# Reordering the opening of a gated attention kernel: K(2) ahead of score(1), a copy given to VectorE, and loads and stores moved between the queues

## The chip, the cores and the metric

The kernel runs on one core of one Trainium2 chip. The metric is the time of one execution on the device in microseconds (us), the median over several executions; lower is better. Engine names in the profile: PE is TensorE, with PEld for its weight loads, DVE is VectorE, ACT is ScalarE, POOL is GpSimd, SP is the engine that here only issues DMAs.

## The reference, cut to what matters

`x` and `ctx` are 4 x 512 rows of 512 numbers, float32. Attention here runs over the 16 heads of one and the same token, not over tokens: for every token a 16 x 16 score matrix is formed.

```python
def attn(q, k, v):                       # 16 heads of 32
    Q = (q @ Wq.T + bq).reshape(bs, sl, 16, 32)
    K = (k @ Wk.T + bk).reshape(bs, sl, 16, 32)
    V = (v @ Wv.T + bv).reshape(bs, sl, 16, 32)
    weight = softmax(einsum('bshd,bsgd->bshg', Q, K), axis=-1)
    return einsum('bshg,bsgd->bshd', weight, V).reshape(bs, sl, 512) @ Wo.T + bo

x = x + tanh(g_xattn[0]) * attn(layernorm(x), ctx, ctx)
w = weight * scale_weight[:, None]
x = x + tanh(g_ffn[0]) * (layernorm(x) @ w.T + bias)
```

## The kernel before, in words

**Tiling.** The 2048 rows are cut into eight chunks of 256 tokens, c = 0 to 7, each of two tiles of 128. Every layer product (K, Q, V, O for the output projection, F for the last layer) keeps float32 precision by splitting both factors into a high and a low part in fp32r: `hi` is the rounded value, `lo` the difference. ScalarE makes the high parts (`high`, L718), VectorE or GpSimd the low ones (`low`, L911). A product is high x high, then the two mixed terms, 12 matmuls per output block. K and Q come out transposed (`cols_layer`, L510: two blocks of two groups, 48 matmuls of 256 columns), V, O and F as rows (`rows_layer`, L499: two tiles of 12 matmuls of 512 columns). All of them share the two PSUM banks `acc[0]` and `acc[1]`: a layer may start on a bank only when the layer before has been read out of it (`bank_free`, L480).

**Per chunk.** K and Q are written to DRAM scratch and read back in another layout (`save_k`, `load_k`, `save_q`, `load_q`, L324 to L352), K is laid out once more by ScalarE (`lay_keys`, L781), V goes through DRAM too (`save_v`, `load_v`, L368 to L384). `score(c)` (L606) is 128 small matmuls and needs the loaded Q and the laid K. VectorE then turns the scores and does the softmax (`scores_turn`, `softmax_a`, `softmax_b`), with the exponential on ScalarE, and `spread_first` (L1034 on) spreads the weights over a block diagonal; GpSimd or ScalarE does the rest of the spread. `attend(c)` (L624) is 128 small matmuls on it. Their result is copied out of PSUM in 16 copies of 32 x 256, 8 for each tile (`attn_copy`, L787, ScalarE; for the last chunk VectorE helps in `attn_some`, L1059), split into high and low (`attn_high`, `attn_low`), and used by O. `o_residual` (L1079) adds the residual and frees the bank; it waits for the output bias that GpSimd adds to the residual rows (`res_bias`, L1250). The layer norms are `norm_stats` and `norm_apply` on VectorE with a small power on GpSimd (`root`, L1239); `turn_x1` and `turn_x2` transpose their results on TensorE.

**Order.** Each engine has its own instruction stream, and the order in it is written out by hand: a prologue, then `tensor_step(i)`, `scalar_step(i)`, `vector_step(i)` and `pool_step(i)` for i = 0 to 8, steps 2 to 5 in a loop. An engine works strictly in its order; a wait holds up all that is behind it. The engines meet at semaphores only. The parts that matter here:

- TensorE (L652 to L703): 12 warming matmuls, K(0), V(0) with the transposes of x(0) between its tiles, Q(0), half of K(1), the transposes of x(1), the rest of K(1), half of Q(1). Step 0: score(0), the rest of Q(1), V(1), attend(0), transposes of x(2). Step 1: score(1), K(2), O(0), Q(2), attend(1), transposes of x2(0), V(2), F(0). O(0) puts its result into the banks that K(2) has left, Q(2) takes the banks that O(0) has left, F(0) those that V(2) has left.
- ScalarE (L821 to L904): in step 0 exp(0), half of Q(1)'s bias, the issue of Q(1)'s store (L872), the spread, ctx(2)'s high part, lay_keys(1), tanh, x(2)'s high part, copies of attention(0)'s first tile and its high part, half of K(2)'s bias; in step 1 the copies of the second tile come first.
- VectorE, `second_step` (L1116 on): scores and first half of softmax(1), low part of attention(0)'s tile 0, the two bias rows multiplied by tanh, second half of the softmax, x(2)'s low part, attention(0)'s tile 1, the spread, o_residual(0) and the second layer norm, the scaling of the F weights, norm of x(3), `x1_apply(3)` (L945), the low parts of F's weights and of x2(0), then `v_bias(2)` (L990), which frees the bank for F(0).
- GpSimd (`pool_step`): in step 0 the root for x(2) and `res_bias(0)`, which waits for both scaled bias rows; in step 1 `spread_last(1)`, two roots, one more root, `x2_bias(0)`, which waits for both low parts of x2(0), `res_bias(1)`, ctx(3)'s low part.
- SP (L400 to L437): all loads and stores, in one queue in written order.

## Time and profile before

| | |
|---|---|
| median of 3 runs | 281.3 us |
| lowest and highest | 280.01 and 281.74 us |
| the profiled execution's own time | 281.8 us |
| its span in the trace | 280.1 us |
| TensorE matmul busy | 267.5 us, 96% of the span |
| VectorE, ScalarE, GpSimd busy | 198.8, 144.5 and 88.4 us |
| DMA | 53.83 MB, mean 192 GB/s |

The profiled execution lies 0.5 us above the median, and 1.7 us of its time lie outside the span. Times in rows are from the span's start. A row of a timeline gives the start, the time from first start to last end, the engine, the line, the instruction, what it writes and reads, how often, and in brackets how long the engine had been idle before and what ended that.

### The profile page before, as it was taken

To read this page: it belongs to the slowest core of one execution; us is meant where nothing else is said; L and a number is where in the kernel's file an instruction comes from. 1 tells how busy PE (TensorE), PEld (TensorE's weight loads), DVE (VectorE), ACT (ScalarE), POOL (GpSimd) and SP (SyncE) were. 2 spreads that over 40 slices of the span, in tenths; PEclk is the share of its full clock that TensorE was granted. 3 is DMA by queue.
4 is the path that set the end of the run, shared out by engine and by line. 5 is a ranking of instruction groups with operands and counts; after the bars stand their busy time and mean duration, and the time that the engine had idled before them with its cause. 6 is when DMAs were issued, how large, how long until landed. Compare 5 with 4: busy or idle time off the path is not lost.

```text
span 280.1 us, 8653 instructions
## 1 busy us (share of the span) xinstructions
PE 267.5 (96%) x3516; PEld 235.9 (84%) x3516; DVE 198.8 (71%) x331; ACT 144.5 (52%) x276; POOL 88.4 (32%) x80
## 2 busy tenths in 40 slices
PE   7899998498999999999999999999999999999995
PEld 7789997397978898888988899889988998887775
DVE  2775569189885987569774987579773855598884
ACT  4755543853686236643387225933289432954700
POOL 4104000032157116422183024612183031802722
PEclk9999999899999999999999999999999999999999
DMA  6997769991887764894488853986478729263203
GB/s 204 351 382 226 208 247 249 258 232 56 274 248 237 147 225 150 235 220 139 160 232 247 191 195 130 240 225 156 181 201 246 158 77 231 74 128 72 104 37 112
DMA packets 71912, 53.83 MB, mean 192 GB/s; under 512 B 36688, under 2 KB 59984, under 8 KB 71888
## 3 DMA queue, kind: packets, MB, share of 16 engines
q1 hardware_dynamic: 71744, 52.97, 65.6%
q10 hardware_dynamic: 144, 0.52, 0.5%
q8 instruction: 17, 0.28, 0.4%
q14 instruction: 7, 0.06, 0.1%
HBM read 34.08 MB, written 19.40 MB: 191 GB/s over the span
## 4 chain that ended last, share of the span: by engine, by line
PE 69%; DMA 10%; SPq 7%; ACT 7%; DVE 3%; issue 3%; DVEq 0%; ACTq 0%
PE acc L496 55%; PE score_ps L496 4%; PE score_ps L616 3%; DMA raw_spare<-wq_t 3%; ACT late L796 3%; PE attn_ps L638 3%; PE turn_ps L530 2%; DMA v_scratch<-v_or_norm 2%; SPq L350 2%; DMA k_rows<-k_scratch 2%; DMA q_pad<-q_scratch 2%; SPq L398 1%; SPq L335 1%; DVE turned L1002 1%; DMA q_scratch<-q_t 1%
## 5 line engine op out<-in xcount | busy, mean ns | idle before, releaser
L796 ACT ACTIVATE late<-attn_ps 32x256 f32<-32x256 f32 x124 | 46.6, 376 | 6.1 <-PE attn_ps L638 3.2
L496 PE MATMUL acc<-ctx_parts,wk_parts 128*128 128x256 f32 x384 | 48.7, 285 | 0.3 <-DVE late L1079 0.2
L496 PEld LDWEIGHTS acc<-ctx_parts,wk_parts 128*128 128x128 f32 x384 | 47.1, 191 | 1.7 <-issue 0.8
L1242 POOL TENSOR_TENSOR rstd<-var_eps,minus_half 128x1 f32<-128x1 f32 (+1 forms) x24 | 17.5, 728 | 95.3 <-DVE var_eps L937 95.3
L496 PE MATMUL acc<-wv_parts,ctx_parts 128*128 128x512 f32 x192 | 46.0, 394 | 0.8 <-ACT wv_parts L720 0.8
L496 PEld LDWEIGHTS acc<-wv_parts,ctx_parts 128*128 128x128 f32 x192 | 35.4, 188 | 8.1 <-issue 1.0
L496 PE MATMUL acc<-xa_parts,wq_parts 128*128 128x256 f32 x336 | 41.1, 281 | 0.1
L496 PE MATMUL acc<-wo_parts,xa_parts 128*128 128x512 f32 x168 | 40.4, 395 | 0.6 <-ACT xa_parts L720 0.6
L496 PEld LDWEIGHTS acc<-xa_parts,wq_parts 128*128 128x128 f32 x336 | 40.2, 188 | 0.7 <-DVE xa_parts L913 0.5
L496 PEld LDWEIGHTS acc<-wo_parts,xa_parts 128*128 128x128 f32 x168 | 31.0, 188 | 7.9 <-ACT xa_parts L720 1.0
L496 PE MATMUL acc<-wf_parts,x_parts 128*128 128x512 f32 (+1 forms) x132 | 29.7, 380 | 0.1
L770 ACT ACTIVATE q_t<-acc,bq_col 128x256 f32<-128x256 f32 x32 | 13.4, 470 | 29.6 <-PE acc L496 29.5
L496 PEld LDWEIGHTS acc<-wf_parts,x_parts 128*128 128x128 f32 x132 | 24.0, 188 | 5.2 <-issue 0.5
L1253 POOL TENSOR_TENSOR x_res<-x_res,bo_row 128x512 f32<-128x512 f32 x16 | 22.0, 1397 | 17.0 <-DVE bf_row L1123 16.8
L1266 POOL TENSOR_TENSOR spread<-probs_t,same_token 128x768 f32<-128x768 f32 x6 | 10.1, 1685 | 49.2 <-DVE probs_t L1032 49.2
L770 ACT ACTIVATE k_t<-acc,bk_col 128x256 f32<-128x256 f32 x32 | 13.3, 471 | 21.5 <-PE acc L496 21.3
L784 ACT ACTIVATE k_keys<-k_rows 128x1024 f32<-128x1024 f32 x8 | 16.5, 2062 | 12.8 <-DMA k_rows<-k_scratch 12.8
L1071 DVE SCALAR_TENSOR_TENSOR late<-acc,tanh_g,late 128x512 f32<-128x512 f32 (+1 forms) x11 | 8.0, 726 | 18.3 <-PE acc L496 18.3
L1247 POOL TENSOR_TENSOR ctx_parts<-ctx_raw,ctx_parts 128x1024 fp32r<-128x1024 f32 x6 | 14.5, 2425 | 19.0 <-ACT ctx_parts L720 19.0
L1259 POOL TENSOR_TENSOR late<-late,bf_row 128x512 f32<-128x512 f32 x14 | 19.1, 1380 | 4.5 <-DVE x_parts L913 3.5
L1002 DVE STREAM_TRANSPOSE turned<-score_ps 128x512 f32<-128x512 f32 x16 | 10.5, 694 | 11.9 <-PE score_ps L616 11.6
L751 ACT ACTIVATE probs<-probs 128x512 f32<-128x512 f32 x8 | 5.1, 632 | 23.8 <-DVE probs L1017 23.8
(89 smaller groups left out, 377.7 us busy)
## 6 DMA issues: line engine op xcount, KB each, us to landing
ctx_raw<-ctx_t SPq DMA_DIRECT2D x8, 512.0 KB, 4.7
x_norm<-x SPq DMA_DIRECT2D x8, 512.0 KB, 5.2
k_scratch<-k_t SPq DMA_DIRECT2D x8, 512.0 KB, 3.7
k_rows<-k_scratch SPq DMA_DIRECT2D x32, 128.0 KB, 3.4
q_pad<-q_scratch SPq DMA_DIRECT2D x32, 128.0 KB, 3.2
v_scratch<-v_or_norm SPq DMA_DIRECT2D x32, 128.0 KB, 2.2
v_keys<-v_scratch SPq DMA_DIRECT2D x16, 256.0 KB, 4.3
x_res<-x SPq DMA_DIRECT2D x8, 512.0 KB, 3.8
```

What stands on the lines that cost most here:

```text
L496: last = pe.matmul(dst, left(a, k), right(b, k), start=(n == 0), stop=(n == len(terms) - 1))
L616: last = pe.matmul(score_ps[r][HD * pair:HD * (pair + 1), ROWS * o:ROWS * (o + 1)], k_keys[half, n:n + 2].rearrange("p s g -> p (s g)"), q ...
L638: last = pe.matmul(attn_ps[HD * t:HD * (t + 1), BANK * r + ROWS * eight:BANK * r + ROWS * (eight + 1)], v_keys[half, EIGHTS * t + eight, : ...
L770: nc.scalar.activation(dst[:, :, m, :], acc[m // 2][:, TOK * (m % 2):TOK * (m % 2 + 1)].rearrange("p (t n) -> p t n", t=GROUPS), ACT.Ident ...
L784: nc.scalar.activation(k_keys[:].rearrange("p n (m q) -> p n m q", q=QH), k_rows[:].rearrange("p q m n -> p n m q"), ACT.Identity).then_in ...
L796: nc.scalar.activation(attn_rows(t, q), attn_block(t, q), ACT.Identity).then_inc(a_out, 1)
L1002: nc.vector.transpose(by_half[:, b].rearrange("p e (s x) -> p e s x", s=2), score_ps[b][:].rearrange("p (e x s) -> p e s x", x=HT, s=2)).t ...
L1242: nc.gpsimd.tensor_tensor(rstd[which][:, t], var_eps[which][:, t], minus_half[:, t], ALU.pow).then_inc(n_rstd[which], count)
L1247: nc.gpsimd.tensor_tensor(ctx_parts[:, LO], ctx_raw[:], ctx_parts[:, HI].bitcast(F32), ALU.subtract).then_inc(ctx_lo, 1)
L1253: nc.gpsimd.tensor_tensor(x_res[:, t, :], x_res[:, t, :], bo_row[:], ALU.add).then_inc(res_biased, 1)
L1259: nc.gpsimd.tensor_tensor(x2_of(c)[:, t, :], x2_of(c)[:, t, :], bf_row[:], ALU.add).then_inc(x2_biased, 1)
L1266: nc.gpsimd.tensor_tensor(spread[:, first:].rearrange("p o h t -> p (o h) t"), probs_t[:, first:].rearrange("p o h -> p (o h)").unsqueeze( ...
```

## The change

It has six parts.

1. TensorE: K(2) runs ahead of score(1), behind the transposes of x(2), where it was behind score(1).
2. Attention(0)'s second tile is copied out of PSUM by VectorE (8 copies), in VectorE's step 0. ScalarE copies the first tile as before, and then lays K(1), takes x(2)'s high part, K(2)'s bias and the second tile's high part, all in step 0.
3. Start: x(0) is loaded behind the two halves of wv. VectorE takes x(0)'s statistics behind the low parts of wv. The transposes of x(0) stand 4 matmuls inside V(0)'s second tile. Q(0) waits for x(0)'s high part at its start, and for the low part at the first term with it.
4. ScalarE issues V(0)'s four stores and, later, its two loads; SP issues Q(1)'s store, which was ScalarE's. On SP K(1)'s store and loads stand before ctx(2)'s load.
5. The two bias rows are loaded behind Q(1)'s loads, and VectorE multiplies them with tanh behind softmax(1), directly ahead of the spread.
6. F(0): the low part of its weights is waited for inside the first tile; on VectorE the low parts of x2(0)'s tiles stand around that of the second half of F's weights, and `x1_apply(3)` stands behind all of them, ahead of `v_bias(2)`.

```diff
@@ groups_of
+            if first(c):
+                owner = "act" if tile == 0 else "dve"
+                return range(tile * each, (tile + 1) * each) if engine == owner else ()
@@ SP
-            load_x(0)
             for j in range(2):
                 load_w(WV, j)
+            load_x(0)
...
             save_k(0)
             load_x(1)
-            for row, dram in ((bo_row, bo), (bf_row, bf)):
-                sp.dma_start(row[:], dram.partition_broadcast(P)).then_inc(consts_in, DMA)
             load_k(0)
             save_q(0)
             sp.wait_ge(zeroed, 1)
             load_q(0)
+            save_k(1)
             load_x(2)
+            load_k(1)
             load_ctx(2)
-            save_v(0)
-            save_k(1)
-            load_v(0)
-            load_k(1)
+            save_q(1)
             load_q(1)
+            for row, dram in ((bo_row, bo), (bf_row, bf)):
+                sp.dma_start(row[:], dram.partition_broadcast(P)).then_inc(consts_in, DMA)
             load_res(0)
@@ TensorE
-                    if t_done and t == 1:
-                        t_done()
...
+                def within(t):
+                    if t_done and t == 1:
+                        t_done()
+                rows_layer(ctx_parts, "wv", v_mm, high_ready, within,
...
-                    pe.wait_ge(x1_lo, TILES * (c + 1))
+                    pe.wait_ge(x1_hi if first(c) else x1_lo, TILES * (c + 1))
...
+                    if first(c) and t == 0:
+                        pe.wait_ge(w_hi, pieces_to(WF, 1))
...
+                if first(i - 1):
+                    k_layer(2, "v", 1)
                 score(i)
...
                 elif first(i - 1):
-                    k_layer(2, "v", 1)
@@ ScalarE
             for j in range(3):
                 w_high(WK, j)
+            w_high(WV, 0)
             act.wait_ge(biases_in, 2 * DMA)
             k_bias(0, (0,))
-            w_high(WV, 0)
...
             ctx_high(1)
+            act.wait_ge(v_out, TILES)
+            for half in range(2):
+                for r in range(2):
+                    part = 2 * half + r
+                    act.dma_start(v_halves(0)[r].rearrange("(t h n) d -> h n t d", t=TILES, h=2)[half],
+                                  v_rows[HD * part:HD * (part + 1)]).then_inc(v_saved, DMA)
             q_bias(0, (0,))
...
             q_bias(1, (0,))
+            act.wait_ge(v_saved, V_SAVED)
+            for r in range(2):
+                act.dma_start(v_keys[ROWS * r:ROWS * (r + 1)], v_halves(0)[r].rearrange(
+                    "(o e) (g d) -> (e g) o d", e=ROW_TOK, d=HD)).then_inc(v_in, DMA)
...
                     q_bias(1, (1,))
-                    act.wait_ge(q_out, KC * 2)
-                    act.wait_ge(q_moved, DMA * GROUPS)
-                    act.dma_start(q_scratch[:], q_t[:].rearrange("p t m n -> p (t m n)")).then_inc(q_saved, DMA)
                     spread_some(i)
                     ctx_high(2)
-                    lay_keys(1)
                     act.wait_ge(gates_in, 2 * DMA)
                     nc.scalar.activation(tanh_g[:], gates[:], ACT.Tanh).then_inc(gates_done, 1)
-                    x1_high(2)
                     attn_copy(0, 0)
                     attn_high(0, 0)
-                    k_bias(2, (0,))
+                    lay_keys(1)
+                    x1_high(2)
+                    k_bias(2)
+                    attn_high(0, 1)
                     return
-                if first(i - 1):
-                    attn_copy(0, 1)
-                    attn_high(0, 1)
-                    k_bias(2, (1,))
@@ VectorE
                 v_bias(1, 0)
+                ctx_low(2)
                 v_bias(1, 1)
-                ctx_low(2)
+                attn_some(0, 1)
+                attn_low(0, 0)

             def second_step():
                 scores_turn(1)
                 softmax_a(1)
-                attn_low(0, 0)
+                attn_low(0, 1)
+                turned_lo(xa_parts, x1_hi, x1_lo, 2)
+                softmax_b(1)
                 dve.wait_ge(consts_in, 2 * DMA)
                 dve.wait_ge(gates_done, 1)
                 for row, n in ((bo_row, 0), (bf_row, 1)):
                     nc.vector.tensor_scalar(row[:], row[:], tanh_g[:, n:n + 1], None, ALU.mult).then_inc(rows_scaled, 1)
-                softmax_b(1)
-                turned_lo(xa_parts, x1_hi, x1_lo, 2)
-                attn_low(0, 1)
                 spread_first(1)
...
                 w_low(WF, 0)
+                turned_lo(x2_parts, x2_hi, x2_lo, 0, (0,))
+                w_low(WF, 1)
+                turned_lo(x2_parts, x2_hi, x2_lo, 0, (1,))
                 x1_apply(3)
-                w_low(WF, 1)
-                turned_lo(x2_parts, x2_hi, x2_lo, 0)
                 v_bias(2, 0)
```

The counts of ScalarE's and VectorE's copies that later waits compare with are shifted to match.

## Rows read from the trace of the kernel before

**Rows 1.** Timeline of TensorE: start us, us, instruction, count

```profile
13.71 2.97 PE L496 MATMUL acc<-wv_parts,ctx_parts 128*128 128x512 f32 x12 [0.80 <-ACT wv_parts L720]
...
20.36 5.90 PE L496 MATMUL acc<-xa_parts,wq_parts 128*128 128x256 f32 x48
...
46.74 1.50 PE L638 MATMUL attn_ps<-spread,v_keys 64*32 64x64 f32 x128 [0.92 <-DMA v_keys<-v_scratch]
...
53.42 1.95 PE L616 MATMUL score_ps<-q_pad,k_keys 64*32 64x64 f32 x128 [4.16 <-DMA q_pad<-q_scratch]
55.30 6.71 PE L496 MATMUL acc<-ctx_parts,wk_parts 128*128 128x256 f32 x48
...
68.38 5.80 PE L496 MATMUL acc<-xa_parts,wq_parts 128*128 128x256 f32 x48
...
76.40 5.74 PE L496 MATMUL acc<-wv_parts,ctx_parts 128*128 128x512 f32 x24
82.23 5.71 PE L496 MATMUL acc<-wf_parts,x_parts 128*128 128x512 f32 x24
87.87 1.59 PE L616 MATMUL score_ps<-q_pad,k_keys 64*32 64x64 f32 x128
```

**Rows 2.** Windows: stretch, length, busy us by engine, PE clock, DMA share, GB/s

```profile
49.30:53.40 4.10, 0.00 (x0) 0.01 (x1) 0.16 (x1) 3.75 (x7) 0.00 (x0) 1.00 1.06 284
...
55.40:57.00 1.60, 1.60 (x8) 1.60 (x9) 1.57 (x3) 0.87 (x2) 0.00 (x0) 0.50 0.93 261
```

**Rows 3.** DMA issues of the first 95 us: count, KB, median us to landing

```profile
x_norm<-x SPq DMA_DIRECT2D x5, 512.0 KB, 5.6
```

**Rows 4.** Timeline of GpSimd, four stretches

```profile
12.71 1.54 POOL L1242 TENSOR_TENSOR rstd<-var_eps,minus_half 128x2 f32<-128x2 f32 x1 [8.66 <-DVE var_eps L937]
...
26.28 0.70 POOL L1242 TENSOR_TENSOR rstd<-var_eps,minus_half 128x2 f32<-128x2 f32 x1 [2.35 <-DVE var_eps L937]
...
59.63 2.53 POOL L1253 TENSOR_TENSOR x_res<-x_res,bo_row 128x512 f32<-128x512 f32 x2 [16.82 <-DVE bf_row L1123]
...
81.56 3.06 POOL L1259 TENSOR_TENSOR late<-late,bf_row 128x512 f32<-128x512 f32 x2 [3.45 <-DVE x_parts L913]
...
108.68 2.72 POOL L1259 TENSOR_TENSOR late<-late,bf_row 128x512 f32<-128x512 f32 x2
```

**Rows 5.** Timeline of VectorE, four stretches

```profile
12.47 2.35 DVE L913 TENSOR_TENSOR wv_parts<-late,wv_parts 128x1024 fp32r<-128x1024 f32 x2
...
44.46 1.76 DVE L1041 TENSOR_TENSOR spread<-probs_t,same_token 128x1536 f32<-128x1536 f32 x1
...
55.39 1.31 DVE L1002 STREAM_TRANSPOSE turned<-score_ps 128x512 f32<-128x512 f32 x2 [5.93 <-PE score_ps L616]
...
65.48 1.48 DVE L1049 TENSOR_TENSOR spread<-probs_t,same_token 128x1280 f32<-128x1280 f32 x1
66.88 0.74 DVE L1079 SCALAR_TENSOR_TENSOR late<-acc,tanh_g,x_res 128x512 f32<-128x512 f32 x1
...
78.15 1.00 DVE L950 TENSOR_SCALAR raw_spare<-x_norm,moments,rstd 128x512 f32<-128x512 f32 x2 [0.59 <-POOL rstd L1242]
...
80.20 1.28 DVE L913 TENSOR_TENSOR x_parts<-turn_ps,x_parts 128x512 fp32r<-128x512 f32 x2
81.40 1.46 DVE L996 TENSOR_TENSOR v_or_norm<-acc,bv_row 128x512 f32<-128x512 f32 x2
...
108.75 2.93 DVE L950 TENSOR_SCALAR raw_spare<-x_norm,moments,rstd 128x512 f32<-128x512 f32 x2 [0.88 <-POOL rstd L1242]
```

**Rows 6.** Timeline of ScalarE

```profile
49.60 1.93 ACT L784 ACTIVATE k_keys<-k_rows 128x1024 f32<-128x1024 f32 x1 [2.62 <-DMA k_rows<-k_scratch]
...
76.08 3.14 ACT L796 ACTIVATE late<-attn_ps 32x256 f32<-32x256 f32 x8
79.25 1.09 ACT L720 ACTIVATE x_parts<-turn_ps 128x512 fp32r<-128x512 f32 x2
```

**Rows 7.** Operations on attn_ps: count, ns minimum, median, maximum, first and last start

```profile
L1065 DVE COPY late<-attn_ps x4: 419/421/423, 259.6 to 261.0; 32x256 f32<-32x256 f32 x4
```

27 lines of the change are left out of this document (16 added, 11 removed).

## The prediction

> **What bounds the kernel now.** I began with the table of busy shares (TensorE 96% of the span) and the waits of TensorE. Its largest is that of score(1) on Q's loads. The timeline of TensorE places it: attend(0) starts at 46.74 after 0.92 idle, score(1) at 53.42 after 4.16, and at the start V(0) had waited 0.80 [rows 1]. From F(0) at 82.23 on, TensorE works almost without a gap to the end, so what counts is one number: when F(0) starts. The windows show a second price of the long wait: the clock reads 1.00 while TensorE idles and 0.50 (1.2 GHz) after it resumes [rows 2]. Score(1) took 1.95 instead of 1.59, K(2) 6.71 instead of the 5.80 of Q(2), of the same shape [rows 1]: 0.36 + 0.91 = 1.3 us.
>
> Then the engines that feed it. The landing of x is 5.6 us [rows 3]. GpSimd and VectorE read differently together than apart: the root at 12.71 took 1.54 us beside VectorE's low parts (from 12.47), the one at 26.28 only 0.70; and `x1_apply` took 1.00 us at 78.15 with GpSimd idle, 2.93 at 108.75 beside the 2.72 of `x2_bias` from 108.68 [rows 4, 5]. One of the two stands still behind the other. Last, ScalarE (lay_keys 1.93, 8 copies 3.14 [rows 6]) and a copy on VectorE (0.42 [rows 7]).
>
> **Start (parts 3, 4).** x(0), issued behind wv, gives wv the queue: half a megabyte less ahead of it. I take V(0)'s 0.80 wait as gone, V(0) at 12.95. VectorE takes x(0)'s statistics only behind the low parts of wv, about 14.0 instead of 10.6. Statistics 2.0 (10.6 to the root at 12.71), root 0.70 (VectorE is idle now [rows 4]), first apply 0.55 with latencies: about 17.5. TensorE has done tile 0 and four matmuls at 16.7 (12 matmuls are 2.8 us [rows 1]), so it waits 0.8 there. Q(0) starts at 20.3 against 20.36 [rows 1]. The sum of the start is 0; ends: -0.7 if x lands early and nothing waits, +0.9 if the root takes 1.54 again.
>
> ScalarE's six DMA issues lie where it waited before (V(0)'s store, from 22.8, up to the bias of Q(0), the loads behind Q(1)'s first half). I take nothing, bounds 0 and +0.5, from a store's issue of 0.4 us four times against about 1 us of free time. V(0)'s loads leave at about 37 and, with the 5.6 of x for a landing [rows 3], are there at 43. Then attend(0) waits for the spread alone, 44.46 + 1.76 = 46.22 [rows 5]: it starts at 46.27, gain 0.47. Bounds 0 and 0.92 [rows 1].
>
> **K(2) ahead of score(1) (parts 1, 2).** From Q(2)'s start to V(2)'s are 8.02, of which Q is 5.73 and attend with its transposes 2.29 [rows 1]; so K(2) can start at 46.27 + 2.29 = 48.56. It needs ctx(2)'s high part, which ScalarE makes when V(1) has ended (46.74 - 0.92 = 45.8), about 1.1 long like the 1.09 of as many elements [rows 6]: 47.1 with latencies. VectorE's low part follows (1.2, half of 2.35 [rows 5]), now ahead of V(1)'s second bias: 48.9, used at 49.0. K(2) runs at full clock, 5.7: 54.25. Score(1) needs lay_keys(1): copies from 47.8 (attend(0)'s end), 3.14, high part 0.6, lay_keys 1.93 [rows 6] = 53.5, covered by 0.7. VectorE's eight copies at 0.445 from start to start are 3.6 [rows 7], 49.5 to 53.1, in a hole of 5.93 us [rows 5]: free. Score(1) takes 1.5: it ends at 55.8 instead of 55.4.
>
> So the 4.16 wait, 1.3 of clock and 0.47 are removed and K(2)'s 5.7 us are done earlier. But Q(2) needs the bank that `o_residual(0)` frees, and that hangs on the softmax of score(1). Before, K(2) and O(0) covered it; now O(0) alone. O(0) ends at 61.4. VectorE, from score(1)'s end: transposes, peak, subtraction 2.7; low parts 1.8; second softmax half 2.5; both bias rows 0.8: 7.8 in all, each link with its start-to-start time of the same timeline, so the spread starts at 63.6. Before, from the transposes at 55.39 to the spread at 65.48 were 10.1 [rows 5]; 1.2 less of waiting for exp and about 1 of waiting behind GpSimd make up the difference.
>
> **The bias rows (part 5).** GpSimd may add the bias to the residual only when both rows are scaled. Before, that was at 59.6, 7 us ahead of use [rows 4, 5]. Now it comes at the moment at which the spread starts on VectorE. If GpSimd stands still behind the spread (1.48 [rows 5]), as the root did behind the low part at 12.5, then half of 2.53 = 1.27 [rows 4] follows: `o_residual(0)` starts at 63.6 + 1.48 + 1.27 + 0.1 = 66.4, else at 65.0. With its 0.74 Q(2) starts at 67.2, against 68.38 before: 1.2 earlier is all that is left. TensorE has then been idle for 5.8 us. The only long idle time in the trace dropped the clock, so I add a slow stretch again: 1.6 (bounds 0.9, what K(2) lost alone, and 1.8, half of the 3.6 us from 53.42 [rows 1] to 57.0, up to where the window shows 0.50 [rows 2]). Q(2) ends at 74.5, against 74.11: +0.4.
>
> At 12.71 VectorE had started first and GpSimd was the one held: 12.47 + 1.18 + 0.6 = 14.25, just the end of its 1.54. The Trainium skill ("SBUF — State Buffer", section "Who interferes with whom") says the same for two kinds of VectorE instructions, those with two SBUF inputs and the fast single-input modes, and that the second to start blocks fully. By that rule the sum is the one here, and 1.3 lower at Q(2) without it.
>
> **F(0) (part 6).** Before, the eight copies of attention(1)'s first tile started 1.97 behind Q(2)'s end (76.08 [rows 6] less 68.38 + 5.73). Now: 74.5 + 1.8 = 76.3, the ends of q_bias and of F's second high part, no idle time between. Copies 3.14, first half of 1.09 [rows 6] with latency 0.6: x2(0)'s first high part at 80.0. Before, VectorE used this time for `x1_apply(3)` (78.15) and F's second low part, and v_bias(2) came right behind x2(0)'s low parts, at 81.40 [rows 5]. Now VectorE idles from about 77 to 80 and then has in front of v_bias(2): 0.6 + 1.15 + 0.65 = 82.4, and `x1_apply(3)`. The second low part of x2(0) is also what releases GpSimd's `x2_bias` (81.56, right behind 80.20 + 1.28 [rows 4, 5]). So `x1_apply(3)` and `x2_bias(0)` start together: 1.0 alone, 2.93 at worst [rows 5]; one of the two tiles held is 2.1 (1.0 and one `x2_bias` tile of 1.36, less some 0.3 that VectorE's own first tile covers), which I take. v_bias(2) 0.7: F(0) starts at 82.4 + 2.1 + 0.7 = 85.2. The ends are 84.1 and 86.1. V(2) has ended at 82.5; a wait of 2.7 stands ahead of F(0), where 0.09 was. Waits of 0.9 kept the clock and 4.16 lost it, so here it may fall too: 0 to +1.2, taken as 0.
>
> **Sum.** F(0) starts at 85.2 against 82.23: +3.0. Nothing behind it gets shorter; x(3) goes to DRAM 2 to 3 us later, with slack of about as much until VectorE turns it, taken as 0. The profiled execution would become 281.8 + 3.0 = 284.8; it lies 0.5 above the median, so 284.3 as a median of runs, 1.1% slower. About 1% is what a measurement of this kernel can tell from no change.
>
> **Rivals.**
> A. No collision: GpSimd does not hold the residual up, `x1_apply(3)` takes 1.0, the clock falls little. Q(2) then starts at 65.9 and ends at 71.7 to 73.3, the copies at 74.4 to 75, high part at 78.2 to 78.7, F(0) at 82.2 to 82.7. 0 to +0.5: 281.3 to 281.8, no change. For it: at both places the two start within some 0.1 to 0.2 us of each other (GpSimd at 81.56, where the VectorE rows end at 81.48), so a little decides. Against it: in the rows GpSimd and VectorE lengthen each other every time they meet.
> B. The saving stays: what is removed (4.16 + 1.3 + 0.47 = 5.9) is not given back, or half of it, 278 to 275.4. It decides if `o_residual(0)` is ready within 6 us of score(1)'s end; for it speaks that 11.5 us of the old order (55.39 to 66.88 [rows 5]) held work that has moved away. Against it: what is left there is a chain of 9 us on one engine.
> C. ctx(2) or K(1) comes late. ctx(2)'s load is now behind K(1)'s loads, about 39.5, where it was at 32. Landing of the same size is 5.6 [rows 3], 45.1, against a need at 46. Beyond 46.6 it moves score(1) nearly one for one, and all behind it. At 2 us late: 286.
>
> **How the numbers follow.** Forecast 0.55, A 0.22, B 0.10, C 0.13. The forecast's own spread is F(0) from 84.1 to 86.1 and 0.5 for score(1), 282.8 to 286.0; 0.36 of its 0.55 lies above 284.1, the 1% line. Slower by over 1%: 0.36 + 0.11 of C = 0.47. Faster: B, 0.10. Within: 0.43. The range 280.6 to 286.4 leaves out B and the far end of C and of the slow clock, 0.2 in all.
>
> **What would show it.** Right: no wait ahead of score(1) and K(2) ahead of it; a wait of 5 to 6 us of TensorE ahead of Q(2), released by VectorE's L1079, and the clock at 0.50 after it; `res_bias(0)` longer than 2.53; `x1_apply(3)` at 1.5 to 2.9 and a wait of 2 to 3 us ahead of F(0). Wrong: Q(2) before 66, or F(0) before 83.5. The start is judged by Q(0) at 20.3, C by ScalarE's high part of ctx(2) later than 46.6.

## The result, and the profile after

| | before | changed |
|---|---|---|
| median, first comparison | 280.83 us (280.01 to 281.74, 4 executions) | 289.35 us (287.01 to 291.13, 4 executions) |
| ratio, 95% interval | | 1.0281 [1.0233, 1.0329] |
| the profiled execution, its span, mean clock | 281.8, 280.1 us | 287.01, 285.3 us, 0.988 |

The changed kernel is 2.8% slower, where 1.1% had been predicted: the sign is right, and the time lies 3 us above the range. The same kernel was measured twice more, beside the experiments: 285.63 us, 1.0167 [1.0120, 1.0214], and 285.95 us, 1.0176 [1.0115, 1.0236]. So a loss of some 1.7% came back each time, inside the predicted range, and about 1% was there in the first comparison alone. A ratio leaves out every execution more than 1.5% above the fastest of its kernel, so below it can differ from the quotient of two medians.

The mean granted clock of the single executions explains a part of this. The kernel before ran 279.1 to 279.9 us at a mean clock of 1.00 and, but for two executions of 284.2 and 286.6, 280.8 to 283.2 at 0.988; one more, of 327.2 at 0.754, stands apart. The changed one, in its twelve executions, ran 284.6 to 286.4 at 0.999 and 1.00, 285.0 to 287.0 at 0.988, 288.0 at 0.982, and 287.1, 290.7 and 291.1 at 0.975 and 0.976. So 5 to 7 us are there at the same full clock, and in some executions a clock that fell in more stretches comes on top. The mean clock does not settle a time by itself: at 0.975 and 0.976 the times still lie 4 us apart.

The timeline of TensorE of the changed kernel (columns as in [rows 1]):

```profile
13.50 3.87 PE L502 MATMUL acc<-wv_parts,ctx_parts 128*128 128x512 f32 x16
17.96 1.11 PE L536 MATMUL turn_ps<-ident,x_norm 128*128 128x128 f32 x8 [0.60 <-DVE x_norm L984]
...
20.76 6.07 PE L502 MATMUL acc<-xa_parts,wq_parts 128*128 128x256 f32 x48
...
47.62 1.50 PE L652 MATMUL attn_ps<-spread,v_keys 64*32 64x64 f32 x128 [1.07 <-DMA v_keys<-v_scratch]
...
49.89 5.88 PE L502 MATMUL acc<-ctx_parts,wk_parts 128*128 128x256 f32 x48
55.71 1.59 PE L628 MATMUL score_ps<-q_pad,k_keys 64*32 64x64 f32 x128
57.23 1.67 PE L502 MATMUL acc<-wo_parts,x_parts 128*128 128x512 f32 x6
60.57 4.38 PE L502 MATMUL acc<-wo_parts,x_parts 128*128 128x512 f32 x18 [1.68 <-issue]
68.63 7.45 PE L502 MATMUL acc<-xa_parts,wq_parts 128*128 128x256 f32 x48 [3.68 <-DVE late L1098]
...
86.59 7.08 PE L502 MATMUL acc<-wf_parts,x_parts 128*128 128x512 f32 x24 [2.58 <-issue]
93.60 1.59 PE L628 MATMUL score_ps<-q_pad,k_keys 64*32 64x64 f32 x128
```

Against [rows 1]: attend(0) starts 0.88 later (47.62 for 46.74) and waits 1.07 for `v_keys` where it waited 0.92; K(2) and score(1) run without a wait; the 4.16 us wait of before has become one of 3.68 ahead of Q(2) and one of 2.58 ahead of F(0), with a stop of 1.68 inside O(0) besides. F(0) starts 4.36 later (86.59 for 82.23) and takes 1.37 longer, so score(2) starts 5.73 later. Of that the rest of the kernel gives back half a microsecond: the span is 5.2 longer.

Most of the 0.88 is older than attend(0). VectorE's spread, which attend(0) needs too, starts at 45.15 for 44.46 [rows 5], 0.69 later, and ScalarE's last high part of wk had started 0.78 later, ahead of all that the change moved (first the kernel before, then the changed one):

```profile
8.37 1.06 ACT L720 ACTIVATE wk_parts<-spread 128x1024 fp32r<-128x1024 f32 x1 [0.78 <-DMA spread<-wk_t]
```

```profile
9.15 1.06 ACT L733 ACTIVATE wk_parts<-spread 128x1024 fp32r<-128x1024 f32 x1 [0.75 <-DMA spread<-wk_t]
...
45.15 1.76 DVE L1060 TENSOR_TENSOR spread<-probs_t,same_token 128x1536 f32<-128x1536 f32 x1
```

That part of `wk` starts anywhere from 8.12 to 9.82 in the profiles below, and Q(0) from 20.13 to 21.41; in the second repeat of the changed kernel Q(0) starts at 20.14.

The windows behind the two waits, columns as in [rows 2], show the clock falling both times:

```profile
68.60:70.00 1.40, 1.37 (x8) 1.40 (x9) 1.21 (x4) 0.00 (x0) 1.40 (x2) 0.64 0.22 72
70.00:72.00 2.00, 2.00 (x11) 2.00 (x11) 1.77 (x5) 0.00 (x0) 1.03 (x3) 0.50 0.22 24
...
86.60:88.00 1.40, 1.40 (x3) 1.12 (x4) 1.40 (x2) 1.33 (x4) 1.40 (x2) 0.50 0.82 320
```

0.50 is the 1.2 GHz level. Q(2) took 7.45 us instead of 5.80, F(0) 7.08 instead of 5.71.

GpSimd of the changed kernel, against [rows 4]. The root of x(0) no longer meets VectorE (0.71 for 1.54); `res_bias(0)` now meets the spread (3.66 for 2.53):

```profile
16.62 0.71 POOL L1263 TENSOR_TENSOR rstd<-var_eps,minus_half 128x2 f32<-128x2 f32 x1 [12.56 <-DVE var_eps L956]
...
65.18 3.66 POOL L1274 TENSOR_TENSOR x_res<-x_res,bo_row 128x512 f32<-128x512 f32 x2 [21.68 <-DVE bf_row L1146]
...
84.10 2.92 POOL L1280 TENSOR_TENSOR late<-late,bf_row 128x512 f32<-128x512 f32 x2 [5.12 <-DVE x_parts L932]
```

VectorE of the changed kernel, against [rows 5]. `o_residual(0)` waits 1.23 for GpSimd; `x1_apply(3)` starts 0.16 ahead of GpSimd's `x2_bias(0)` and takes 1.96 instead of 1.00, with `v_bias(2)`, which frees F(0)'s bank, right behind it:

```profile
65.02 1.48 DVE L1068 TENSOR_TENSOR spread<-probs_t,same_token 128x1280 f32<-128x1280 f32 x1
67.73 0.75 DVE L1098 SCALAR_TENSOR_TENSOR late<-acc,tanh_g,x_res 128x512 f32<-128x512 f32 x1 [1.23 <-POOL x_res L1274]
...
81.59 0.69 DVE L932 TENSOR_TENSOR x_parts<-turn_ps,x_parts 128x512 fp32r<-128x512 f32 x1 [3.17 <-ACT x_parts L733]
...
83.94 1.96 DVE L969 TENSOR_SCALAR raw_spare<-x_norm,moments,rstd 128x512 f32<-128x512 f32 x2
85.81 1.27 DVE L1015 TENSOR_TENSOR v_or_norm<-acc,bv_row 128x512 f32<-128x512 f32 x2
```

So the wait ahead of F(0), which the timeline calls "issue", is one for `v_bias(2)`'s first half: F(0) follows 0.78 behind its start.

The DMA queues and issues from 30 to 48 us (queue: packets, MB, share of the 16 engines; then count, KB, median us to landing):

```profile
q1 hardware_dynamic: 2243, 3.14, 59.0%
q10 hardware_dynamic: 4128, 0.52, 20.0%
...
v_keys<-v_scratch ACTq DMA_DIRECT2D x2, 256.0 KB, 8.4
k_rows<-k_scratch SPq DMA_DIRECT2D x4, 128.0 KB, 4.7
ctx_raw<-ctx_t SPq DMA_DIRECT2D x1, 512.0 KB, 8.1
```

Queue q10, ScalarE's, carries V(0)'s half megabyte in 4128 packets, some 127 bytes each, beside q1, SP's. The two loads left at 36.4 and 37.1 and the slower one landed after 10.3 us, at 47.5. Before, SP issued them 4 us later, at 40.4, and they landed after 3.7 and 5.4. They were sent earlier and arrived later.

### The profile page after: what moved, and what is told of

It is laid out like the page before. It is cut to its first block, busy times and chain, and to the rows that moved or that the text cites. A ratio compares the mean times of both kernels' runs of the same rounds, so it can differ in the third digit from the quotient of the medians.

```text
span 285.3 us, 8652 instructions
## 1 busy us (share of the span) xinstructions
PE 269.8 (95%) x3516; PEld 238.1 (83%) x3516; DVE 203.1 (71%) x339; ACT 141.5 (50%) x268; POOL 88.7 (31%) x80
## 4 chain that ended last, share of the span: by engine, by line
PE 77%; DMA 7%; issue 4%; DVE 4%; ACT 3%; SPq 2%; POOL 1%; DVEq 0%; POOLq 0%; ACTq 0%
PE acc L502 62%; PE score_ps L502 4%; PE score_ps L628 4%; PE attn_ps L652 4%; PE turn_ps L536 3%; DMA x_res<-x 3%; DMA late<-wv_t 2%; DMA q_scratch<-q_t 2%; ACT late L809 1%; SPq L342 1%; DVE turned L1021 1%; POOL x_res L1274 1%; ACT k_t L783 1%; SPq L405 1%; DVE peak L1033 1%
## 5 line engine op out<-in xcount | busy, mean ns | idle before, releaser
L502 PE MATMUL acc<-ctx_parts,wk_parts 128*128 128x256 f32 x384 | 47.9, 283 | 0.1
L502 PEld LDWEIGHTS acc<-ctx_parts,wk_parts 128*128 128x128 f32 x384 | 46.6, 189 | 0.9 <-ACT wk_parts L733 0.3
L809 ACT ACTIVATE late<-attn_ps 32x256 f32<-32x256 f32 x116 | 43.6, 376 | 6.5 <-PE attn_ps L652 3.9
L502 PE MATMUL acc<-xa_parts,wq_parts 128*128 128x256 f32 x336 | 42.8, 287 | 3.7 <-DVE late L1098 3.7
L1263 POOL TENSOR_TENSOR rstd<-var_eps,minus_half 128x1 f32<-128x1 f32 (+1 forms) x24 | 16.7, 695 | 95.0 <-DVE var_eps L956 95.0
L502 PEld LDWEIGHTS acc<-xa_parts,wq_parts 128*128 128x128 f32 x336 | 41.8, 195 | 4.4 <-issue 4.1
L502 PE MATMUL acc<-wf_parts,x_parts 128*128 128x512 f32 (+1 forms) x132 | 31.1, 392 | 2.6 <-issue 2.6
L502 PEld LDWEIGHTS acc<-wf_parts,x_parts 128*128 128x128 f32 x132 | 25.0, 196 | 8.1 <-issue 3.0
L783 ACT ACTIVATE q_t<-acc,bq_col 128x256 f32<-128x256 f32 x32 | 13.4, 471 | 36.6 <-PE acc L502 36.4
L1274 POOL TENSOR_TENSOR x_res<-x_res,bo_row 128x512 f32<-128x512 f32 x16 | 23.4, 1484 | 21.8 <-DVE bf_row L1146 21.7
```

Source lines behind the costliest of these rows:

```text
L502: last = pe.matmul(dst, left(a, k), right(b, k), start=(n == 0), stop=(n == len(terms) - 1))
L783: nc.scalar.activation(dst[:, :, m, :], acc[m // 2][:, TOK * (m % 2):TOK * (m % 2 + 1)].rearrange("p (t n) -> p t n", t=GROUPS), ACT.Ident ...
L809: nc.scalar.activation(attn_rows(t, q), attn_block(t, q), ACT.Identity).then_inc(a_out, 1)
L1263: nc.gpsimd.tensor_tensor(rstd[which][:, t], var_eps[which][:, t], minus_half[:, t], ALU.pow).then_inc(n_rstd[which], count)
L1274: nc.gpsimd.tensor_tensor(x_res[:, t, :], x_res[:, t, :], bo_row[:], ALU.add).then_inc(res_biased, 1)
```

## The experiments

Each kernel is the changed one with an edit, all timed against the kernel before on the same chip. Ratios are to it; 1% is 2.8 us. Where parts 5 and 6 are undone, VectorE's orders are; the bias rows' late loads and F(0)'s later wait for its low weights stay.

**The changed kernel again**, unedited, in two more comparisons.

> The changed kernel once more, unedited. Its four executions so far: 287.01, 288.02, 291.13, 290.67 us, with mean granted clocks 0.988, 0.982, 0.975, 0.975. Theory C (clock): each 0.001 of mean clock is 0.57 us of half-rate time, so the slow executions have 14 us of it where the fast has 7, and a trace of a slow one shows one more half-rate stretch, behind an idle stretch of TensorE that the fast one survived. Rival D (data): the slow ones wait longer for transfers or for instructions, and the clock falls only as a consequence of longer idle time. A profile at 0.988 tells nothing new; one at 0.975 should show the extra stretch with the same idle times ahead of it (C) or with longer ones (D).

> The changed kernel once more, for its spread. So far 287.0, 288.0, 291.1, 290.7 in the first four executions and 284.6, 286.6, 286.2, 285.0 in the second four, mean clocks 0.999 to 0.975. Theory C: time against mean clock falls on one line, 284.6 at 0.999, one full half-rate stretch is 0.006 of the mean clock and costs 1 to 1.7 us. Rival: times at equal clock differ by 2 us or more, so that the waits themselves differ between executions.

285.63 and 285.95 us, as told above. The TensorE timeline of the first, at a mean clock of 0.999:

```profile
68.65 5.94 PE L502 MATMUL acc<-xa_parts,wq_parts 128*128 128x256 f32 x48 [3.11 <-DVE late L1098]
...
85.76 5.72 PE L502 MATMUL acc<-wf_parts,x_parts 128*128 128x512 f32 x24 [3.25 <-issue]
```

The waits are the same, and no clock is lost behind them. In this execution the kernel is 5 us slower than the kernel before at a mean clock of 1.00, with no clock lost.

**Part 6's VectorE order undone.**

```diff
                 w_low(WF, 0)
-                turned_lo(x2_parts, x2_hi, x2_lo, 0, (0,))
-                w_low(WF, 1)
-                turned_lo(x2_parts, x2_hi, x2_lo, 0, (1,))
                 x1_apply(3)
+                w_low(WF, 1)
+                turned_lo(x2_parts, x2_hi, x2_lo, 0)
```

> Part 6 undone on VectorE: x1_apply(3) back between the two low parts of F's weights, both low parts of x2(0) behind. Theory: the 2.6 us of idle time ahead of F(0) and the half-rate clock behind it (F(0) took 7.1 instead of 5.7) come from this order alone; F(0) then starts when V(2) ends, with no idle time, and takes 5.7: 4.0 us less, 283.0 in a run like the profiled one, median about 285. Rival: ScalarE's late high part of x2(0) holds F(0) in any order, and the time falls by less than 1.5 us.

281.96 us, 1.0027 [0.9998, 1.0056] in 10 executions. From 1.0167 that is 1.4%, 3.9 us. TensorE:

```profile
84.37 5.60 PE L502 MATMUL acc<-wf_parts,x_parts 128*128 128x512 f32 x24
```

No wait is left ahead of F(0), and its clock is whole. This order is the dearest edit of the change.

**Part 5's order undone**: the two bias rows scaled ahead of the second half of the softmax.

```diff
+                dve.wait_ge(consts_in, 2 * DMA)
...
-                softmax_b(1)
...
+                softmax_b(1)
                 spread_first(1)
```

> Part 5 undone on VectorE: the two bias rows are scaled ahead of the second half of the softmax, as before; their loads stay late. Theory: GpSimd's res_bias(0) then starts about 62 and is not held by the spread, takes 2.6 instead of 3.66, o_residual(0) follows the spread at once, Q(2) starts 1.2 us earlier. The idle stretch ahead of Q(2) is then 2.4 instead of 3.7; if the clock survives that, another 1.7 us: 1.2 to 2.9 less in all. Rival: both rows' loads or the residual's load (7.2 us to land) arrive only then, and Q(2) moves by less than 0.5.

287.26 us as the median of four. The ratio, 1.0129 [1.0037, 1.0220], rests on two of them (283.01 and 286.77 us), and its interval holds the 1.0167 of no edit. In the profiled execution, one of the two longer ones, `o_residual(0)` no longer waited for GpSimd and Q(2)'s wait was 2.89 instead of 3.11, where 2.4 had been expected; F(0) had lost its clock (8.41). Nothing clear comes from this edit alone. **Parts 5 and 6 undone together:**

> Parts 5 and 6 undone on VectorE, the rest as changed. So far: the changed kernel 285.6 in the last call, with part 6 undone 282.0, with part 5 undone 287.3 (its profile shows Q(2) after 2.9 us of idle time instead of 3.1 to 3.7, GpSimd not held, and F(0) after 3.3 with the clock lost). Theory: the two add up; Q(2) starts some 0.8 earlier than with part 6 undone alone, F(0) without idle time: 281.0 to 282, less of a spread since the idle stretch ahead of Q(2) gets under 3 us. Rival: part 5 gives nothing, since VectorE meets GpSimd elsewhere: 282 or more.

283.0 us, 1.0055 [1.0006, 1.0103], no better than part 6 alone. Taking away GpSimd's hold of `res_bias(0)` is not in the time. The two engines still meet in the trace: GpSimd's share of the spread took 2.71, where it took 1.47, and VectorE's beside it 1.71 for 1.48.

**Part 1 undone**: K(2) behind score(1) again, its bias as before.

```diff
-                if first(i - 1):
-                    k_layer(2, "v", 1)
                 score(i)
+                if first(i - 1):
+                    k_layer(2, "v", 1)
```

> Part 1 undone: K(2) behind score(1) again, with ScalarE's exp(1) ahead of the second half of K(2)'s bias. All else as changed. Theory: TensorE idles ahead of score(1) again until Q(1)'s loads have landed (issued 48.7 to 51.6, so about 54.5: 4 us, clock lost), but K(2) covers the softmax and Q(2) starts without waiting, about 67 to 68 instead of 68.6; F(0)'s stall stays. About 0 to 1.5 us less than the changed kernel. Rival: moving K(2) is what costs the 8 us, and the time falls by 4 us or more.

289.32 us, 1.0307 [1.0243, 1.0371]: slower than the 285.63 of the changed kernel beside it, where 0 to 1.5 us less had been expected. TensorE:

```profile
56.01 2.04 PE L628 MATMUL score_ps<-q_pad,k_keys 64*32 64x64 f32 x128 [4.77 <-ACT k_keys L797]
57.98 7.37 PE L502 MATMUL acc<-ctx_parts,wk_parts 128*128 128x256 f32 x48
65.20 5.65 PE L502 MATMUL acc<-wo_parts,x_parts 128*128 128x512 f32 x24
```

The old wait is back ahead of score(1), now for ScalarE's `lay_keys(1)`, which the change put behind the copies, and the slow clock falls on K(2). K(2)'s move is not what costs; with ScalarE in its new order it is needed.

**Parts 4, 5 and 6 undone**: SP stores and loads V(0), ctx(2)'s load ahead of K(1)'s store (SP's side of the edit is shown).

```diff
-            save_k(1)
             load_x(2)
-            load_k(1)
             load_ctx(2)
-            save_q(1)
+            save_v(0)
+            save_k(1)
+            load_v(0)
+            load_k(1)
             load_q(1)
```

> As the kernel with parts 5 and 6 undone, and part 4 undone too: V(0)'s stores and loads and their places back on SP, Q(1)'s store back on ScalarE. Measures part 4: attend(0) waited for v_keys until 47.6 to 49.3 in the four profiles with part 4, until 46.7 before. Theory D: the transfers got in each other's way (one of V(0)'s loads took 10.3 us to land), so attend(0) starts at 46.7 to 47.3 again, but Q(1) and K(1) come later, and score(1), now behind K(2), waits a little: about -0.5 to +0.5 against the kernel with parts 5 and 6 undone. Rival: attend(0) is late for another reason (the start is 0.4 later, too) and stays at 47.5 or later.

280.87 us, 0.9969 [0.9946, 0.9993]. From 1.0055 that is 0.9%, 2.4 us, for part 4, and the two intervals do not overlap; a change of -0.5 to +0.5 us had been expected. Attend(0) starts at 47.36 and waits 0.54 for the spread.

**Which half of part 4?** Both kernels have parts 5 and 6 undone. In the first only V(0)'s two loads go back to SP, ahead of K(1)'s loads; in the second ScalarE keeps them and only x(2)'s and ctx(2)'s loads go ahead of K(1)'s store.

```diff
             load_x(2)
+            load_v(0)
             load_k(1)
...
-            for r in range(2):
-                act.dma_start(v_keys[ROWS * r:ROWS * (r + 1)], v_halves(0)[r].rearrange(
-                    "(o e) (g d) -> (e g) o d", e=ROW_TOK, d=HD)).then_inc(v_in, DMA)
```

> As the kernel with the VectorE orders of parts 5 and 6 undone (283.0, ratio 1.0055), and in addition V(0)'s two loads issued by SP instead of ScalarE, directly ahead of K(1)'s loads; the stores stay with ScalarE. Theory (the loads land late because a second queue, with its packets of 128 bytes, shares the DMA engines with the large transfers of SP's queue): issued behind about 36.5 they land within 4 to 6 us, about 42, K(1)'s loads leave some 2 us later, attend(0) waits for the spread at most (0.5, start 47.0 to 47.5), and the ratio falls to 0.997 to 1.001. Rival (the loads are slow because ctx(2)'s and Q(1)'s transfers lie beside them, whatever the queue): the landing stays at 8 to 10 us, attend(0) waits over 1 us for v_keys, the ratio stays at 1.004 to 1.008.

281.07 us, 0.9988 [0.9965, 1.0010], 12 executions. Its issues from 30 to 48 us, and its attend(0):

```profile
v_keys<-v_scratch SPq DMA_DIRECT2D x2, 256.0 KB, 5.3
```

```profile
46.67 1.50 PE L653 MATMUL attn_ps<-spread,v_keys 64*32 64x64 f32 x128 [0.46 <-DVE spread L1057]
```

```diff
-            save_k(1)
             load_x(2)
-            load_k(1)
             load_ctx(2)
+            save_k(1)
+            load_k(1)
             save_q(1)
```

> As the kernel with the VectorE orders of parts 5 and 6 undone (283.0, ratio 1.0055), and in addition x(2)'s and ctx(2)'s loads ahead of K(1)'s store on SP, as in the kernel before; ScalarE still issues V(0)'s stores and loads. Theory (two queues): ctx(2) is away from beside the loads, but K(1)'s loads and Q(1)'s store are not; the landing falls to 6 to 8 us, about 44, attend(0) waits at most 0.5, ratio 0.998 to 1.002. Rival (V's loads are slow on ScalarE's queue whatever lies beside them): landing 8 to 10 us, attend(0) waits 1 us and more, ratio 1.004 to 1.008.

280.64 us, 0.9973 [0.9953, 0.9994], 12 executions:

```profile
v_keys<-v_scratch ACTq DMA_DIRECT2D x2, 256.0 KB, 6.7
```

```profile
46.66 1.50 PE L652 MATMUL attn_ps<-spread,v_keys 64*32 64x64 f32 x128 [0.56 <-DVE spread L1060]
```

With either edit attend(0) waits for the spread alone, and 0.7 to 0.8% comes back, the 0.7 with an interval that just touches that of the 1.0055. All the profiles together say of V(0)'s two loads:

| | profiles | the slower one lands after | attend(0) starts behind the spread's end by |
|---|---|---|---|
| part 4 as changed | 10 | 10.3 to 12.2 us | 0.66 to 2.50 us |
| order of before (the kernel before; part 4 undone) | 6 | 5.1 to 5.7 | 0.10 to 0.90 |
| the first cure (loads by SP, ahead of K(1)'s) | 1 | 6.0 | 0.10 |
| the second cure (ctx(2)'s load ahead) | 1 | 7.6 | 0.10 |

The second cure keeps ScalarE's queue and takes away the company: ctx(2)'s load had left before, and K(1)'s leave at 40.7 instead of 37.4. So that queue by itself does not make the loads land after 10 us. The first takes away both: V(0)'s loads go ahead of K(1)'s in one queue, and ctx(2)'s leaves at 42.4 instead of 39.3, when V(0)'s have landed (36.2 + 6.0). Whether the same company on one queue would do the same harm was not tried. The first cure has a price of its own: ctx(2) arrives at 47.9, and K(2) stops 0.52 for its low part. And the order of before is no full cure, since its loads are quick but leave at about 41: in three of the five kernels that restored it attend(0) waited 1.1 to 1.3 for `v_keys`.

The Trainium skill ("DMA: Bandwidth & Descriptors", section "Issuing engines are not separate DMA queues") says that DMAs of all issuing engines run on the same 16 DMA engines and interleave there, and that issuing from a second engine saves only the time to issue. The traces agree: moving the loads to ScalarE bought no transfer time, and what it put side by side shared the engines.

**Only parts 1 and 2 left**: 3 to 6 undone.

> Parts 3, 4, 5 and 6 undone: the kernel before with K(2) ahead of score(1) and the copy on VectorE only (and the bias rows' loads late, F's low-part wait late). Measures part 3, for which I had taken 0; the changed kernel's profiles have Q(0) at 20.1 to 21.4 against 20.36 before. Theory: without part 3 Q(0) starts at 20.4 and the time is 0 to 0.5 less than with parts 4 to 6 undone, ratio 0.996. It also is the test of rival B of the prediction, that K(2)'s move itself gains: ratio under 0.99 would say so. Rival: part 3 gained, and the ratio rises to 0.999 or more.

281.32 us, 0.9988 [0.9953, 1.0023]. Score(1) has no wait and Q(2) has one of 2.87: the move of K(2) and the copies on VectorE show no gain by themselves. Part 3 shows none either: with it (0.9969) and without it (0.9988) the intervals overlap over more than half their length; Q(0) started at 20.91 and 21.11.

**GpSimd behind `x1_apply(3)`**: one wait added ahead of `x2_bias(0)`, so that the two don't run together.

```diff
+                        pool.wait_ge(n_done[0], 4 * TILES)
```

> The changed kernel; GpSimd's x2_bias(0) waits for x1_apply(3), too. My prediction's term: the two start together and hold each other up, x1_apply(3) takes 1.96 in the changed kernel's profile instead of 1.00. Theory: with GpSimd behind, it takes 1.0, v_bias(2) and F(0) come 0.95 earlier, and x2_bias(0) has slack enough: 0.9 us less, 284.7 where the changed kernel has 285.6, or more if the idle stretch, then 2.3 us, keeps the clock. Rival: x1_apply(3) stays at 2 us, or GpSimd's delay shows up elsewhere and nothing is gained.

Its VectorE and then its GpSimd:

```profile
83.97 0.99 DVE L969 TENSOR_SCALAR raw_spare<-x_norm,moments,rstd 128x512 f32<-128x512 f32 x2
84.88 1.28 DVE L1015 TENSOR_TENSOR v_or_norm<-acc,bv_row 128x512 f32<-128x512 f32 x2
```

```profile
85.09 2.98 POOL L1280 TENSOR_TENSOR late<-late,bf_row 128x512 f32<-128x512 f32 x2 [6.09 <-issue]
```

`x1_apply(3)` fell from 1.96 to 0.99, `v_bias(2)` came 0.93 earlier, and so did F(0), at 85.66, again 0.78 behind it. That settles the mechanism, and that F(0)'s wait is one for `v_bias(2)`. The median did not show it: 286.12 us, 1.0157 [1.0069, 1.0245], an interval that holds the unedited kernel's ratio.

**Unread matmuls in the waits.** Two kernels have small matmuls added whose result nobody reads, to keep TensorE at work: 14 ahead of Q(2) and 10 ahead of F(0) in the changed kernel, and 12 ahead of Q(2) with parts 4 to 6 undone.

```diff
+                    pe.wait_ge(s_turned, 4)
+                    keep_clock(7)
                     q_layer(2, "o", 0)
```

> The changed kernel with seven idle-filling 128 x 128 float32 matmuls between O(0) and Q(2) and five ahead of F(0), whose results nobody reads; nothing else moves, and the waits for VectorE stay. It measures what the half-rate clock costs. Theory C: the executions then all are like the one with mean clock 0.999: Q(2) takes 5.8 and F(0) 5.7 after waits that end at the same time, 284.5 to 285.5, with a spread under 1.5 us, where the changed kernel ran from 284.6 to 291.1. Rival: the spread of the changed kernel comes from transfers, and stays at 3 us or more.

286.1 us, 1.0174 [1.0138, 1.0210]: 284.65 and 285.68 at mean clocks of 0.999 and 1.00, 286.53 at 0.993, but also 290.57 at 0.976. One of the four is still as long as the longest without them, so the expected narrowing did not come.

> The kernel with parts 4, 5 and 6 undone (0.9969 of the time before, interval 0.9946 to 0.9993; its profile shows 3.23 us of idle time ahead of Q(2) and Q(2) at 8.63 instead of 5.8), with six unread 128 x 128 matmuls put into that idle stretch once the scores are turned. Theory C: Q(2) keeps the clock in every execution; those at 0.994 move to 1.000, 0.5 to 1.5 us less, ratio 0.992 to 0.995. Rival: the matmuls, 3 us of light work, don't keep the clock or only move the loss to a later stretch, as the 290.6 us execution of the changed kernel with such matmuls suggests; ratio 0.996 or more.

281.18 us, 0.9982 [0.9951, 1.0013], as without them. In the profiled execution the slow clock had only moved, to the stop inside O(0):

```profile
61.45 6.00 PE L503 MATMUL acc<-wo_parts,x_parts 128*128 128x512 f32 x18 [2.88 <-issue]
...
68.54 5.94 PE L503 MATMUL acc<-xa_parts,wq_parts 128*128 128x256 f32 x48
```

**The stop inside O(0)**: the loads of the scale row and of F's weights put behind V(1)'s loads, in a single execution.

> The changed kernel with the loads of the scale row and of F's weights behind V(1)'s loads. In every profile with K(2) ahead, O(0) stops after its sixth or so matmul for 1.4 to 2.3 us, with no releaser in the profile; in the second in which it stops, 58 to 59, one 16 KB packet of an instruction queue is in the trace, and the 16 DMA engines are at 100% with the loads of F's weights. Theory I: TensorE waits for its next instructions, which stand behind data packets; with the data loads later the stop shrinks to under 1 us. Rival: it waits for a semaphore that the profile does not name, and the stop stays at 1.4 to 2.3. Neither changes the time by more than 0.5, since Q(2) waits for VectorE anyway: 284 to 288 for one execution.

287.62 us once. The stop of 1.41 us ended at 60.82, and the DMA engines were 19% busy from 59 to 60 and idle from 60 to 61; with the loads in place it was 1.68. Under 1 us had been expected if the loads made it. In this one execution the stop lasted on without traffic on the DMA engines, so traffic is not needed for it.

**K(2) in halves around score(1).** Three tries to fill both waits: half of K(2) ahead of score(1), half behind it. The first, with parts 5 and 6 undone, lays K(1) ahead of the spread on ScalarE.

> Parts 5 and 6 undone, and K(2) split: its first half ahead of score(1), the second behind it, with lay_keys(1) moved ahead of the spread on ScalarE. If both covers count, 2.9 us of K(2) shorten the wait ahead of score(1) (Q(1)'s loads land about 54) to about 1.5 to 2 us, and 2.9 us of K(2) with O(0) cover VectorE's 10 us chain from score(1) to o_residual(0) but for 1.5 us. No idle stretch over 2.5 us, clock kept: Q(2) starts about 66.5 instead of 68.6, 279 to 280.5, faster than both kernels. Rival: Q(1)'s loads land later than that or O(0) waits for ScalarE, and the time stays at 281 or more.

281.1 us, 1.0001 [0.9975, 1.0027]. O(0) runs without a stop and Q(2) waits 2.09, but attend(0) waits 2.61 for ScalarE's part of the spread, now behind `lay_keys(1)`: one wait exchanged for another. The second, with part 4 undone too, lays K(1) behind the spread and ahead of the copies.

> From the kernel with parts 4, 5 and 6 undone (280.9, against 281.6 before in the same call): K(2) split, first half ahead of score(1), second behind it; on ScalarE lay_keys(1) and the bias of K(2)'s first half ahead of attention(0)'s copies. In the split tried before, lay_keys(1) ahead of the spread on ScalarE made attend(0) 1.9 us late. Theory: score(1) then starts about 53.5 with at most 2 us of idle time ahead, K(2)'s second half and O(0) end about 63.7, o_residual(0) is ready at 65 to 65.5: Q(2) starts at 65.5 with under 2 us of idle time, the clock is kept, F(0) starts about 79.5: 278 to 279.5, faster than before by 1% or nearly. Rival: F(0) is held by VectorE's and ScalarE's work for F's weights at 81 or later, and the time stays at 280 or more.

282.63 us, 1.0057 [1.0025, 1.0089]. The order was at fault: VectorE stood at a low part of attention(0) until 58.6 (for 4.81 us), so score(1)'s transposes began only at 59.4, and Q(2) waited 3.28. The third is the second with both low parts of attention(0) behind the first half of the softmax, x(2)'s low part behind the second, and x(2)'s high part behind the exponential on ScalarE (the edit in part, against the changed kernel):

```diff
+                if first(i - 1):
+                    k_layer(2, "v", 1, (0,))
                 score(i)
+                if first(i - 1):
+                    k_layer(2, "v", 1, (1,))
...
+                    lay_keys(1)
+                    k_bias(2, (0,))
                     attn_copy(0, 0)
...
+                attn_low(0, 0)
                 attn_low(0, 1)
-                turned_lo(xa_parts, x1_hi, x1_lo, 2)
...
+                turned_lo(xa_parts, x1_hi, x1_lo, 2)
                 spread_first(1)
```

> The half-and-half K(2) again, with what its first form had wrong: there VectorE's low part of attention(0)'s first tile stood ahead of the scores and waited for ScalarE until 58.6, so the softmax began 3.6 us late. Here both low parts stand behind softmax_a, and on ScalarE x(2)'s high part behind exp(1). Theory: score(1) ends at 55.8 as there, o_residual(0) is ready 10.5 us later at 66.3, Q(2) starts about 66.5 with 2 us of idle time, clock kept, 1.1 us ahead of the kernel with parts 4 to 6 undone and 1.5 to 2 more from the clock: ratio 0.990 to 0.995. Rival: K(1)'s loads, which landed at 52.1, move score(1) beyond 54.5, ratio 0.997 or more.

280.16 us (279.16 to 281.40, 12 executions), 0.9951 [0.9920, 0.9981]: the fastest version here, 0.5% under the kernel before. In the same comparison two kernels with all of K(2) ahead, that of parts 1 and 2 and the one with 12 unread matmuls, ran 281.32 and 281.18 us. Its interval overlaps those of 0.9969 and 0.9973, which also lie under 1. TensorE:

```profile
53.76 1.58 PE L629 MATMUL score_ps<-q_pad,k_keys 64*32 64x64 f32 x128 [0.90 <-DMA q_pad<-q_scratch]
55.26 3.08 PE L503 MATMUL acc<-ctx_parts,wk_parts 128*128 128x256 f32 x24
...
59.80 4.49 PE L503 MATMUL acc<-wo_parts,x_parts 128*128 128x512 f32 x19 [0.30 <-issue]
66.79 5.87 PE L503 MATMUL acc<-xa_parts,wq_parts 128*128 128x256 f32 x48 [2.50 <-DVE late L1096]
...
86.84 1.59 PE L629 MATMUL score_ps<-q_pad,k_keys 64*32 64x64 f32 x128
```

The 4.16 us wait is shared out as 0.90 and 2.50, neither followed by a slow clock here, and score(2) starts 1.0 earlier than before (86.84 for 87.87).

## Why the prediction was right in sign and short in size

**From attend(0) on the chain of the prediction holds.** It is set beside the trace of the first comparison after adding the 1.35 us that attend(0) came late (47.62 for the predicted 46.27):

| | predicted | + 1.35 | measured |
|---|---|---|---|
| K(2) | 48.56 | 49.9 | 49.89 |
| spread | 63.6 | 64.95 | 65.02 |
| `o_residual(0)` | 66.4 | 67.75 | 67.73 |
| Q(2) | 67.2 | 68.55 | 68.63 |
| F(0) | 85.2 | 86.55 | 86.59 |

The shift alone puts F(0) beyond the 86.1 at which the sum's spread ended.

**The step that failed** is "with the 5.6 of x for a landing [rows 3], are there at 43. Then attend(0) waits for the spread alone, ... gain 0.47". The loads left when predicted, at 36.4 and 37.1, and the slower took 10.3, and up to 12.2 in other profiles with part 4. The 5.6 came from x's loads. The packet size was not what it missed: the same loads, in the same small packets, had landed in 3.7 and 5.4 in the kernel before. The change itself laid K(1)'s loads and ctx(2)'s load beside them on the other queue. I counted the issues that were moved and not what would now be in the air together. The bounds, 0 and a gain of 0.92, had no end on the side of a loss. In this profile the step cost 0.66 of the 1.35 (attend(0) at 47.62, 0.71 behind the spread's end instead of 0.05); in the second repeat it cost 2.45. Undoing part 4 brought 2.4 us, and either cure took the wait for the loads away. The same 5.6 was put in for ctx(2)'s load, which took 8.1.

Rival C named the same stretch and the same direction, but another transfer. Its mark was met: ScalarE's high part of ctx(2) began at 47.34, later than 46.6. It did not bind, because attend(0) was late as well and K(2) found both parts ready. In the first cure, where attend(0) was early, it did bind.

**The term that was mis-sized** is the clock behind F(0)'s wait, "0 to +1.2, taken as 0". In the profiled execution it was +1.37, beyond that bound. With the late attend(0) this accounts for the profile: 3.0 + 1.35 + 1.37 = 5.7, and score(2) starts 5.73 later. In the two later measurements of the changed kernel the profiled executions kept the clock at both places, and 4.6 and 4.7 us of loss remained in the medians. There the slow stretch of 1.6 at Q(2), which the sum contains, was missing too; in the first repeat that brought F(0) only 0.83 forward (85.76 for 86.59), since its wait grew to 3.25. That these medians lie within 1.7 us of the forecast of 284.3 is thus in part luck. The excess of the first comparison, 3.9 us more, goes with mean clocks of 0.975 in two of its four executions; but 287.06 us at 0.976 stands among the repeats. Why the first comparison lost so much stays open: the long executions were not profiled.

**Right:** the saved wait was given back. TensorE ended O(0) at 64.95 and stood until `o_residual(0)` had freed a bank at 68.6; what had covered that chain was K(2). I predicted a wait of 5.8 there. It was 3.68, because O(0) itself ended 3.55 later than predicted, of which its stop, which no term held, is 1.68 and attend(0) 1.35. Rival B, that the saving stays, is refuted by the kernel with parts 1 and 2 alone (0.9988).

**Right:** the mutual hold of VectorE and GpSimd, at both places: `res_bias(0)` 3.66, where 2.53 + 1.27 = 3.8 follows from the text, and `x1_apply(3)` 1.96 for 2.1. The second was tested by separating the two; what the first costs in time was not shown. The Trainium skill's rule ("SBUF — State Buffer", section "Who interferes with whom"), that the second to start is blocked, agrees if it is read instruction by instruction: `res_bias(0)` started 0.16 behind the spread and was the one held; `x1_apply(3)` started 0.16 ahead of GpSimd, so that its second tile came behind GpSimd's first and was held in its turn. Rival A fell with it, since its condition was no hold.

**Right, but small:** the price of part 6. A wait of 2.7 ahead of F(0) was predicted, 2.58 measured in the first profile, and 3.25 and 3.31 in those that kept the clock at Q(2). The sum holds some 2.6 us for it; undoing it brought 3.9.

**The start**, taken as 0 with bounds of -0.7 and +0.9. V(0)'s 0.80 wait went, the transposes of x(0) waited 0.60 (0.8 predicted), and Q(0) came 0.40 late. By the spread ahead of attend(0) this had become 0.69, inside the bounds, and it is the other half of the 1.35. As the weights were already 0.78 late and a repeat had Q(0) at 20.14, I put it down to that execution and not to part 3; a single profile of the kernel before can't prove that.

By parts, as far as the runs tell them apart: part 6 costs 3.9 us (1.0167 to 1.0027) and part 4 costs 2.4 (1.0055 to 0.9969), of which the wait ahead of attend(0) is 0.7 in the two traces (1.25 for 0.54); what the rest is was not shown. Part 5's step (1.0027 to 1.0055) is within the intervals. With parts 4 to 6 undone the kernel lies 0.9 us under the one before, and parts 1, 2 and 3 are worth no more than that.

## What to carry to other kernels

When work is moved ahead of a long wait, look for what it used to cover: the wait reappears at the end of the next chain, and it is smaller only by what the chain itself got shorter. Sharing the movable work out between the two waits did better here than moving all of it, in the one of three tries whose other engines were ordered to suit.

When a transfer is given to another queue or sent earlier, list what is in the air beside it in the new order and take its landing time from a row with the same company; a landing time measured in other company, be it of the same packets, is no bound.

An operation put ahead of the one that frees a bank is on the path, however idle its engine was a microsecond before, and a second engine that is released by the same event can lengthen it.
